# Block attention and mixture of experts on one core: the global rows' return, the gathered queries and one row maximum are reordered

## What is computed

```python
q, k, v = heads(h @ Wq + bq), heads(h @ Wk + bk), heads(h @ Wv + bv)
ctx = local_attention(q, k, v)       # block of 128 queries, window of 256 keys
norm = jnp.linalg.norm(q, axis=-1)
_, top_idx = jax.lax.top_k(norm, 62)
idx = concat([0], top_idx, [t - 1])  # 64 queries of each head
qg = take_along_axis(q, idx)
g_ctx = softmax(qg @ k.T / sqrt(32)) @ v   # these 64 see all 1024 keys
ctx = ctx.at[..., idx].set(g_ctx)
```

## Time and profile before

| | |
|---|---|
| median of 3 runs | 896.55 us (890.6 to 898.4) |
| the profiled execution | 902.7 us |
| its span | 901.0 us |
| PE busy | 810.9 us, 90% |
| DVE busy | 576.3 us, 64% |
| ACT busy | 406.3 us |
| POOL busy | 139.6 us |
| mean granted clock of PE | 0.972 |

### The profile page before, as it was taken

One profiled execution on the slowest core, in us unless ns is written; L12 is line 12 of the kernel. 1 busy time (PEld: TensorE's weight loads), 2 busy tenths in 40 slices (PEclk: granted clock), 3 DMA queues, 4 the chain that ended last, 5 costly groups with the idle time before them and its releaser, 6 DMA issues.

```text
span 901.0 us, 13773 instructions
## 1 busy us (share of the span) xinstructions
PE 810.9 (90%) x5060; PEld 659.7 (73%) x5060; DVE 576.3 (64%) x1262; ACT 406.3 (45%) x787; POOL 139.6 (15%) x201
## 2 busy tenths in 40 slices
PE   2999999988878798898789889889999999999994
PEld 1676867766666576676568778689999999887883
DVE  5544996358787465667348863446666667748565
ACT  2423232325455465556544334456666666733120
POOL 4000001220000400121113562100000000012232
PEclk9999999999999899999979999989999999999998
DMA  6697545974865666663206872248777777645444
GB/s 203 187 298 226 167 134 186 260 229 110 231 187 140 172 166 167 178 196 91 67 29 200 291 246 99 82 153 243 214 224 230 220 214 222 200 151 172 156 132 136
DMA packets 117442, 162.38 MB, mean 180 GB/s; under 512 B 17316, under 2 KB 65188, under 8 KB 117376
## 3 DMA queue, kind: packets, MB, share of 16 engines
q1 hardware_dynamic: 113792, 153.54, 56.4%
q0 software_dynamic: 3584, 7.97, 3.1%
HBM read 107.24 MB, written 55.05 MB: 180 GB/s over the span
## 4 chain that ended last, share of the span: by engine, by line
PE 69%; DVE 17%; DMA 4%; issue 4%; ACT 4%; POOL 1%; SPq 0%; DVEq 0%; POOLq 0%; ACTq 0%
PE bank L163 43%; PE wide L163 19%; PE wide L167 4%; PE bank L167 3%; DVE MX L160 2%; DMA H<-scr_oe,FG 2%; DMA scr_v<-vt 1%; DVE SG L160 1%; DVE STC L273 1%; DVE CX L1392 1%; DVE CT L149 1%; DVE XT L149 1%; DVE SIL L149 1%; DVE W13L L149 1%; ACT HH L145 1%
## 5 line engine op out<-in xcount | busy, mean ns | idle before, releaser
L163 PE MATMUL bank<-XT,W13H 128*128 128x256 f32 (+1 forms) x1056 | 244.8, 327 | 3.1 <-DVE XT L149 3.1
L163 PEld LDWEIGHTS bank<-XT,W13H 128*128 128x128 f32 x1056 | 177.6, 193 | 19.4 <-ACT W13H L145 1.9
L163 PE MATMUL bank<-XT,W13L 128*128 128x256 f32 (+1 forms) x528 | 170.9, 324 | 0.0
L163 PE MATMUL wide<-W2H,HH 128*128 128x512 f32 x352 | 117.3, 399 | 3.7 <-DVE CX L1392 3.5
L163 PEld LDWEIGHTS bank<-XT,W13L 128*128 128x128 f32 x528 | 101.4, 192 | 8.3
L160 DVE TENSOR_REDUCE MX<-wide 128x1 f32<-128x192 f32 (+1 forms) x128 | 76.8, 647 | 34.4 <-PE wide L163 31.2
L157 ACT ACTIVATE PT<-bank 128x512 f32<-128x512 f32 x128 | 74.4, 593 | 30.0 <-PE bank L163 28.9
L149 DVE TENSOR_TENSOR SIL<-bank,SIL 128x256 f32<-128x256 f32 (+1 forms) x72 | 36.9, 512 | 74.1 <-ACT SIL L157 73.4
L157 ACT ACTIVATE SIL<-bank 128x256 f32<-128x256 f32 (+1 forms) x72 | 32.6, 453 | 111.2 <-PE bank L163 110.3
L163 PEld LDWEIGHTS wide<-W2H,HH 128*128 128x128 f32 x352 | 67.6, 192 | 19.6 <-DVE CX L1392 5.2
L163 PE MATMUL wide<-W2L,HH 128*128 128x512 f32 x192 | 76.2, 397 | 0.0
(11 more groups left out here) (207 smaller groups left out, 1468.4 us busy)
## 6 DMA issues: line engine op xcount, KB each, us to landing
R<-in_L_ffn_W_dram SPq DMA_DIRECT2D x48, 512.0 KB, 5.0
scr_q<-hl SPq DMA_DIRECT2D x16, 512.0 KB, 4.2
scr_k<-hl SPq DMA_DIRECT2D x16, 512.0 KB, 3.8
R<-in_L_ffn_sw_dram SPq DMA_DIRECT2D x12, 512.0 KB, 5.0
QSe<-scr_q SPq DMA_DIRECT2D x36, 128.0 KB, 3.2
KSe<-scr_k SPq DMA_DIRECT2D x36, 128.0 KB, 3.4
scr_v<-vt SPq DMA_DIRECT2D x16, 272.0 KB, 2.3
R<-_attn_hidden_states_dram SPq DMA_DIRECT2D x16, 256.0 KB, 3.9
```

Source lines behind the costliest of these rows:

```text
L163: return do("pe", lambda g: g.matmul(ps, a, b, start=start, stop=stop, skip_group_check=True), after, mark=mark)
```

## The change

- `global_back` is no transpose any more but a product with `twice`, which is two identities of 64 one above the other; it turns and adds the two halves. It writes to a bank of `ST_`, and `global_finish` only multiplies, twice, with 64 rows each. The wide buffer of `global_values` is given back by ACT's copy.
- The gathered queries are split and turned pair by pair: `stack_split(i+1)` in slot 1 on POOL, `stack_q(i+1)` in slot 6 through a bank of `ST_`. The gathers of batch 1 stand singly in slot 4 of periods 6 to 13, those of batch 0 in steps 36 to 43 of stage 1.
- The fourth row maximum moves from slot 5 to slot 6, and the shift of that head from slot 7 to slot 0 of the next period.
- The search's parts stand in the slots with g % 8 in (0, 5, 6, 7).
- At the program's start POOL clears two `GT` buffers of 64 columns, and DVE makes `twice`.

```diff
+        m_two = do("dve", lambda g: g.tensor_tensor(twice[:, :], ident[:, 0:64], ident[:, 64:128], ALU.add), [m_id])
...
+        for b in GT:
+            m_zgt = do("pool", lambda g, b=b: g.memset(f(b[:, 64:128]), 0.0))
...
+        def stack_split(i):
+
+            gs = GS[i % 2]
+            a1 = copy("pool", gs[:, 32:96].rearrange("p (l d) -> p l d", l=2),
+                      G[:, i, :].unsqueeze(1).broadcast_to([P, 2, HD]),
+                      [gm[i], Q_last(Q, "pool")] + gs_busy[i % 2])
+            stacked[i] = tt(gs[:, 0:32], G[:, i, :], f(gs[:, 32:64]), ALU.subtract, [a1], e="pool")
+
+        def stack_q(i, ring):
+
+            ti, tb, tfree = ring.take()
+            m_t = tr(tb[0:96, 0:P], f(GS[i % 2][:, :]), ident[:, :], [stacked[i], m_id] + tfree, mark=True)
+            gs_busy[i % 2] = [m_t]
+            m_gt[i] = copy("act", GT[i % 2][:, :].rearrange("p (z t) -> p z t", z=3)[:, 0:3:2, :],
+                           tb[0:96, 0:P].rearrange("p (z t) -> p z t", z=2), [m_t] + gt_busy[i % 2])
+            ring.busy[ti].append(m_gt[i])
...
                 m_c = copy("act", os[:, 0:P], w[:, 0:P], [m_o] + sfree)
+                W_.busy[g_["wi"]].append(m_c)
...
-                g_["m_t"] = tr(g_["back"], os[:, 0:P], ident[:, :], [m_c, m_id], mark=True)
+                ti, tb, tfree = ST_.take()
+                g_["back"] = (ti, tb)
+                g_["m_t"] = mm(tb[:, 0:64], os[:, 0:P], twice[:, :], True, True, [m_c, m_two] + tfree, mark=True)
...
-                halves = []
                 for s in range(2):
                     rw = slice(64 * s, 64 * s + 64)
-                    c0 = HD * s
-                    m_c = copy("dve", GC[rw, i, :], w[rw, c0:c0 + HD], [g_["m_t"]])
-                    halves.append(tt(GC[rw, i, :], GC[rw, i, :], w[rw, 64 + c0:64 + c0 + HD], ALU.add, [m_c]))
-                m_f = ts(GC[:, i, :], GC[:, i, :], sg[:, 2:3], None, ALU.mult, None, [m_r] + halves)
+                    m_f = ts(GC[rw, i, :], tb[rw, HD * s:HD * s + HD], sg[rw, 2:3], None, ALU.mult, None,
+                             [m_r, g_["m_t"]])
                 SG.busy[g_["sgi"]].append(m_f)
-                W_.busy[g_["wi"]].append(halves[1])
+                ST_.busy[ti].append(m_f)
...
-            for at, (r, part) in zip([g for g in range(48) if g % 8 in (2, 5, 6, 7)], parts):
+            for at, (r, part) in zip([g for g in range(48) if g % 8 in (0, 5, 6, 7)], parts):
...
-            ROW_MAX = {0: (0, 0), 3: (0, 1), 4: (1, 0), 5: (1, 1)}
+            ROW_MAX = {0: (0, 0), 3: (0, 1), 4: (1, 0), 6: (1, 1)}
...
-                    if g == 1:
-                        stack_q(0)
-                    if k == 1 + late:
+                    if g == 0:
+                        stack_q(0, ST_)
+                    if k == 6 and i < 15:
+                        stack_q(i + 1, ST_)
+                    if k == 4 and 6 <= i < 14:
+                        gather(i + 2)
+                    if k == 1 and 1 <= i < 15:
+                        stack_split(i + 1)
+                    if k == 1:
                         global_scores(i)
-                if k == 7 and i < 15:
-                    row_shift(2 * i + 3, ST_)
+                if k == 0 and 0 < i < 16:
+                    row_shift(2 * i + 1, ST_)
```

More of the change, by code:

```diff
@@ L207, in sandwich @@
         KS0 = [sb(early, f"KSe{i}", [97, SEQ], F32R) for i in range(2)]
+        GS = [sb(early, f"GS{i}", [P, 96], F32R) for i in range(2)]
+        GT = [sb(early, f"GT{i}", [96, 192], F32R) for i in range(2)]
+        twice = sb(early, "twice", [P, 64])
         VS0 = [sb(early, "VSe", [P, 9, 2 * VW])]
@@ L238, in sandwich @@
         IDF = [sb(early, f"IDF{b}", [16, 64]) for b in range(2)]
-        FD = [sb(early, f"FD{b}", [16, 2, 64]) for b in range(2)]
-        FS = [sb(early, f"FS{b}", [16, 2, 64]) for b in range(2)]
-        EQ = [sb(early, f"EQ{b}", [16, 2, 64]) for b in range(2)]
+        FD = [sb(early, "FD", [16, 2, 64])] * 2
+        FS = [sb(early, "FS", [16, 2, 64])] * 2
+        EQ = [sb(early, "EQ", [16, 2, 64])] * 2
         RC = sb(early, "RC", [16, 2])
@@ L319, in sandwich, with gather @@
         gm, m_gt = [], {}
[L321 to L327, removed]
+        def gather(i, after=()):
+            b, g = divmod(i, 8)
+            gm.append(dma("pool", gs_slots[i % 4], lambda e: e.indirect_dma_start(
+                out=G[:, i, :], out_offset=None, in_=qrows[0:(b + 1) * SEQ * HEADS, :],
+                in_offset=bass.IndirectOffsetOnAxis(ap=IG[:, b, g:g + 1], axis=0)),
+                list(after) + [m_ig[b]] + ([gm[i - 4]] if i >= 4 else [])))
+        stacked = {}
+        gs_busy, gt_busy = [[], []], [[], []]
+        def stack_split(i):
[11 more added lines that the diff above has]
+            ring.busy[ti].append(m_gt[i])
         heads, vq = {}, {}
@@ L667, in topk_step @@
                     tp.busy[ti].append(topk_rows(0, tb, tfree))
-                    gather_q(0, qt_b0)
+                if 36 <= u < 44:
+                    gather(u - 36, qt_b0)
+                if u in (45, 46):
+                    stack_split(u - 45)
             def topk_ids(b):
                 F_, D_, S_f, E_ = IDF[b], FD[b], FS[b], EQ[b]
-                a = copy("dve", F_[:, :], TI[b][:, :], [tk[b]["m"]])
+                a = copy("dve", F_[:, :], TI[b][:, :], [tk[b]["m"], m_ig.get(0)])
                 a = do("dve", lambda g: g.memset(F_[:, 62:63], 0.0), [a])
@@ L792, in late_rows @@
                     m_vzero.append(k0)
[L794 to L816, removed]
             ct, ctx_stored, gp = {}, {}, {}
@@ L973, in global_finish @@
                 sg = g_["sg"]
-                w = g_["back"]
+                ti, tb = g_["back"]
                 m_r = do("dve", lambda g: g.reciprocal(sg[:, 2:3], sg[:, 3:4]), [g_["m_e"]])
-                halves = []
                 for s in range(2):
                     rw = slice(64 * s, 64 * s + 64)
-                    c0 = HD * s
-                    m_c = copy("dve", GC[rw, i, :], w[rw, c0:c0 + HD], [g_["m_t"]])
-                    halves.append(tt(GC[rw, i, :], GC[rw, i, :], w[rw, 64 + c0:64 + c0 + HD], ALU.add, [m_c]))
-                m_f = ts(GC[:, i, :], GC[:, i, :], sg[:, 2:3], None, ALU.mult, None, [m_r] + halves)
+                    m_f = ts(GC[rw, i, :], tb[rw, HD * s:HD * s + HD], sg[rw, 2:3], None, ALU.mult, None,
+                             [m_r, g_["m_t"]])
                 SG.busy[g_["sgi"]].append(m_f)
-                W_.busy[g_["wi"]].append(halves[1])
+                ST_.busy[ti].append(m_f)
                 g_["m_f"] = m_f
@@ L1004, in rows_1 @@
                 ST_.busy[ti].append(topk_rows(1, tb, tfree))
[L1005 to L1008 removed]
+            chores = {1: late_rows, 48: lambda: topk_ids(1), 50: rows_1}
             parts = [(r, part) for r in range(8) for part in range(3) if r < 7 or part < 2]
[L1010 removed]
+            for at, (r, part) in zip([g for g in range(48) if g % 8 in (0, 5, 6, 7)], parts):
                 chores[at] = lambda r=r, part=part: topk_part(1, r, part)
[L1012 removed]
             for b in busy13 + busy2:
                 b += begun
[L1016 removed]
+            ROW_MAX = {0: (0, 0), 3: (0, 1), 4: (1, 0), 6: (1, 1)}
             def slot_of(g):
                 i, k = divmod(g, 8)
[L1021 removed]
                 if i < 16:
@@ L1044, in slot_of @@
                     global_finish(i - 1)
-                if k == 1 + late and i < 16:
+                if k == 1 and i < 16:
                     global_max(i)
@@ L1054, in slot_of @@
                     row_max(2 * i + 2 + ROW_MAX[k][0], ROW_MAX[k][1])
-                if i < 16 and 4 <= k - late < 7:
-                    global_turn(i, k - 4 - late)
+                if i < 16 and 4 <= k < 7:
+                    global_turn(i, k - 4)
                 if k == 0 and i > 0:
```

8 lines of the change are left out of this document (3 added, 5 removed).

## The result

| | before | after |
|---|---|---|
| median | 895.25 us (890.6 to 898.4, 4 runs) | 908.83 us (906.76 to 912.27, 4 runs) |
| profiled execution, span | 901.0 us | 910.5 us |
| mean granted clock | 0.972 | 0.954 |

The ratio is 1.016 with a 95% interval of 1.0101 to 1.0219: the change made the kernel slower by about 14 us. The forecast was 888 us, faster. Stage 2, from the first `local_scores` to the first product of stage 3, lasted 263.6 us before (193.11 to 456.70) and lasts 271.6 us now (192.60 to 464.19): 8.0 of the 9.5 us between the two profiled executions lie in stage 2.

A forecast was written before the change was run, and what follows sets the result against it. Periods 1 to 5 were taken as bound by DVE, 7 to 15 by PE. 9.2 + 4.6 + 4.2 - 0.25 - 2.5 - 3 - 3.4 = 8.9 us off the 896.55 us median gave 888 us, range 882 to 893.

The forecast's parts named there:

- Part 1: Periods 1 to 5, DVE's pace: shorter finish and moved search part save 1.85 us a period, 9.2 us.
- Part 2: Periods 8 to 14, PE's pace: wait for `GC` goes, 0.65 us a period, 4.6 us; `PTG` wait stays.
- Rival C: PE's `GC` wait returns at `global_back`'s bank before `local_scores` of slot 4; about 895 us; chance 0.16.
- Part 3: Periods 6, 7, 15 and the last finish: shorter waits and fewer transposes in a row save 4.2 us.
- Part 4: Program start: two more memsets of 64 columns delay POOL's first power; +0.25 us cost.
- Part 5: Entrance to stage 2: PE's longer wait for head 2's row shift lowers its clock; +2.5 us, bounds 0 and 3.5.
- Part 6: Odd head's row shift moves behind twelve loads on SP and lands slightly late; +3 us, bounds 0 and 12.
- Rival B: Odd row shift late every period, PE waits 1 to 1.5 us in 13 periods; 909 us at worst; chance 0.14.
- Part 7: After the store of `h_x1`, an odd row shift goes out 5.5 us later behind twelve loads, once; +3.4 us.

The follow-up runs named there:

- e11: e7 with the search's parts back in the slots with g % 8 in (2, 5, 6, 7); 881.31 us against 875.93 of e7.
- e7: e5 with the loads of values in even periods issued after the even head's row shift; 875.79 us, ratio 0.976; run again 875.93 us, ratio 0.969.
- e3: The kernel before with the new finish alone (`twice`, bank of `ST_`, ACT's copy freeing the wide buffer), small search buffers shared; ratio 0.992, 7.7 us faster.
- e10: e7 with the fourth row maximum back in slot 5 and the odd head's row shift in slot 7; 876.73 us against 875.93 of e7.
- e2: The kernel before with only the fourth row maximum in slot 6 and the odd row shift in the next slot 0; 916.53 us against 905.34, ratio 1.012.
- e4: The changed kernel with the fourth row maximum back in slot 5 and the odd row shift in slot 7; 891.41 us against 905.34, ratio 0.9825.
- e9: The changed kernel with the shared expert's weight loads moved from slot 7 to slot 1 of the next period, behind the odd row shift; ratio 0.997.
- e1: The changed kernel with slot 0's twelve loads of two heads issued after the odd head's row shift; 894.3 us against 905.34, ratio 0.987.
- e8: The changed kernel with the row shifts issued on ACT's queue instead of SP's; ratio 1.000.
- e5: e1 with head 5's loads and the first load of values in period 0 issued after the row shift of head 2; 887.4 us, ratio 0.991.

## Why the prediction was wrong

**Part 1 was right.** Forecast 13.99 us for period 2, measured 14.11. On DVE, at the turns to periods 1 and 2, for the earlier trace rows:

```profile
218.81 0.53 DVE L153 TENSOR_SCALAR GC<-bank,SG 64x32 f32<-64x32 f32 x2
219.38 1.23 DVE L160 TENSOR_REDUCE SG<-wide 128x1 f32<-128x1024 f32 x1
...
220.71 1.21 DVE L160 TENSOR_REDUCE MX<-wide 128x3 f32<-128x768 f32 x2
...
232.22 0.21 DVE L891 RECIPROCAL RS<-bank 128x8 f32<-128x8 f32 x1 [0.43 <-PE bank L167]
```

The two operations take 0.53 us, the reductions of slot 3 follow `SG` at once, and before `RS` 0.43 us of idle time are left of 1.63. e11 bears out the search's share: 5.4 us. Over periods 1 to 5 e7, run again, is 10.0 us shorter than the kernel before (70.8 against 80.8 from the first values of period 1 to those of period 6); 9.2 were forecast.

**Part 2 had the right number, in part by luck.** Period 9 takes 13.58 us, forecast 13.6, before 14.26. But the forecast took all of it from the finish and said that the wait for `PTG` stays. The finish gives 0.44 us there (e3), not 0.65, and with the pairwise queries 14.03 us a period are left (e10). The other 0.45 us come from the late slot, which takes the wait for `PTG` away and which the prediction priced at nothing. The second bank does bring back a small wait (`GC` before a `bank` product, 0.21 us as a rule), not Rival C's.

**Part 3 was too small.** It gave 2.9 us to periods 6 and 7. Before, their values start at

```profile
289.13 1.86 PE bank L163 x20
...
307.79 3.56 PE bank L163 x20
...
325.64 1.86 PE bank L163 x20
```

and they last 18.7 and 17.9 us; in e7, run again, 14.3 and 13.6, which is 8.7 us less. The idle time of 2.47 us and the lower clock of the earlier trace rows are part of this, and the prediction used them only as the price of a stall. POOL issues the eight gathers of batch 1 in a row just then (297.9 to 307.7). The three kernels that do so leave PE idle there for 2.8 to 6.2 us in two or three waits (the kernel before, e2 and e3); in e4, e7 and e9, with single gathers, no idle time of PE in period 6 is over 0.7 us. No run moves the gathers alone, so that they are the cause is not shown.

**Part 4 was right**: POOL's power starts at 7.76 instead of 7.59 us, 0.17 us later where 0.25 was forecast.

**Part 5 was mis-sized.** It gave 2.5 us to low clock and took the landing to be as before. For the earlier trace rows, SP and PE:

```profile
204.15 0.68 SPq L421 DMA_DIRECT2D WQH<-MR  x1
204.87 1.36 SPq L364 DMA_DIRECT2D QSe<-scr_q  x3
```

```profile
209.77 0.80 PE L163 MATMUL bank<-WQH,WKH 97*128 97x256 f32 x2 [6.84 <-DMA WQH<-MR]
```

The transfers ahead of the shift are the same as before, but it takes 5.6 us instead of 3.6, and PE waits 6.84 us. What differs is what follows: before, nothing was issued until the next shift; now the loads of head 6 go out right behind, because no shift holds them back. e1 has the same list ahead and no loads right behind, and there the chain gives that shift 3.98 us. The other kernels with this list ahead and loads right behind have 4.30 (e2) and 4.94 us (e9), so the transfers behind cost 0.3 to 2 us, by one execution each. From the first product of stage 2 to this one went 14.3 us before and 17.2 now: 2.9 us besides the clock, which then makes the 20 products of that period last 3.63 us. The values of period 1 start 3.8 us later than before, counted from the start of stage 2, and the period then takes 15.7 us where e7 takes 14.2: 5.4 us in all instead of 2.5.

**Part 6 was the step that failed.** It rested on "a row shift lands at most 3.5 us after its issue", and it counted the weights by the 0 to 1 us that SP needs to issue them, not by the 1 MB that the engines then have to move. The 3.6 us of the earlier trace rows did come from behind twelve loads and a load of values, but SP had taken 7.3 us to issue these 2.0 MB, time in which most of them could be moved; 1 MB of weights is issued in 1.0 us. The bound was also used for too few periods. Weights stand in slot 7 of periods 2 to 7, so ahead of the rows of periods 3 to 8; the prediction has them for 3 to 5. (A small slip beside it: 9.2 and 3.5 give 12.7 us, not 12.3.)

Measured for these six rows: the shifts went out 10.0 to 13.3 us after the start of the slot 4 before them, where 9.2 to 11 were worked out, and took 5.83, 5.46, 4.92, 5.41, 5.97 and 3.34 us to land. Counted from the first of the weights the landing came 12.5 to 10.8 us later, for 2.5 to 2.0 MB; so it is mostly the volume that sets it, and the last shift is short because it was issued later after its weights than the others. PE waited 2.98, 1.91, 2.00, 0.47, 2.99 and 0.97 us, 11.3 in all. And the price of a wait is not the wait: period 3 is 5.1 us longer than period 2 for a wait of 2.98, period 7 is 5.1 us longer than period 9 for 2.99, since the clock is low after it (1.7 of the other 2.1 us are the 20 products, 3.63 instead of 1.93 us). The forecast was a cost of 3 us with bounds of 0 and 12; by e9 it was 17.0 in periods 3 to 8 alone. This was Rival B, with the wait in nine periods instead of 13, and 0.5 to 5.7 us long instead of 1 to 1.5. Its "909 us at worst" is close to the 908.8 measured.

The Trainium skill ("DMA: Bandwidth & Descriptors", "Queues, rings and completion order") has the rule that a semaphore write waits for every earlier write of its DMA engine, across its queues. I set it beside the sum and took the sum from the 3.5 us. The trace agrees: in the windows above the row lands as the engines run empty. So does e8, where the even head's row, issued on ACT's queue, landed only 7.7 us later behind 2.2 MB issued on SP's. No run here tells this rule from a plain sharing of the engines.

**Part 7 named the right event and missed a larger one.** Period 11 waits 3.42 us behind the store of `h_x1`, where a cost of 3.4 us was forecast; with the low clock after it the period lasts 18.2 us, 4.6 more than period 9:

```profile
375.84 0.33 SPq L776 DMA_DIRECT2D scr_x<-XX  x1
376.22 1.36 SPq L364 DMA_DIRECT2D WQH<-scr_q  x3
```

```profile
386.13 0.80 PE L163 MATMUL bank<-late 97*128 97x256 f32 x2 [3.42 <-DMA late<-MR]
```

But period 10 waits 5.70 us, for a shift that the chain shows from 360.33 to 367.54. The first two `load_tile`, 1 MB in four transfers at 352.9 to 354.7, go out ahead of the twelve loads there, and another tile, a store and values follow behind. I had read those rows only for their place in SP's list. Period 10 takes 20.84 us (355.96 to 376.80), 7.3 more than period 9. Period 12 waits once more, 0.95 us.

**The sum.** The gains were there: from the first `local_scores` to the first product of stage 3 e7, run again, takes 236.1 us, 27.5 less than the kernel before, where 18 were forecast (3.9 of the 27.5 lie ahead of the values of period 1, where the order of e5 and e7 helps too). The costs were put at 9.2 us (0.25, 2.5, 3 and 3.4). The changed kernel takes 271.6 us for the same stretch and differs from e7 in SP's list alone: 35.5 us, of which 28.6 are waits for `MR`; the rest I put down to the clock.

## What to carry to other kernels

A small transfer that an engine waits for must not stand behind bulk, and its delay is set by the volume that the DMA engines still have to move at that moment, weights and stores included, not by the issue time of the queue that it stands in. So when a step with a transfer moves, list the bytes ahead of it and behind it until its use, and fix the list first: here three moves of calls in SP's list turned 1.6% slower into 2.4 to 3.1% faster. Two stalls of PE of 3 us cost 5.1 us each here, for the clock fell; so read the granted clock beside a wait before pricing it. And where two parts of a change move one number, as in part 2, a forecast can hit for the wrong reason: price each apart.

## What the runs showed of the hardware

- A row of 4 KB took 3.6 us from issue to use behind 2.0 MB issued over 7.3 us, 5.8 us behind 2.5 MB issued over 6.7 us, and 7.2 us in period 10, behind 2.5 MB and with 1.5 MB right behind it. From the first of the bulk to the landing of the row it was 10.8 to 12.5 us for 2.0 to 2.5 MB in periods 3 to 8, and 14.6 us in period 10. Issued by ACT's queue behind 2.2 MB of SP's, it took 7.7 us (e8).
- Transfers issued right behind it seem to slow it too: with the same list ahead 4.30, 4.94 and 5.58 us with loads right behind (e2, e9 and the changed kernel), 3.60 and 3.98 us without (the kernel before and e1).
- PE idle for 2.98 us lost its clock (granted 0.62, then 0.50), and worked at 1.2 GHz for the next 20 products: 3.63 instead of 1.93 us for them in period 3. The length of the wait alone does not tell: after waits of 1.85 and 2.46 us in e1 the granted clock stayed at 1.00, after one of 0.76 us in e4, at 270.54, it was 0.50.
- The product of 128 x 64 with `twice` is carried out as two instructions, 0.36 us together, against 0.27 us of the transpose it replaces; nothing waited for it.
